# A two-layer graph attention kernel: the order of work inside a pipeline step is rewritten on three engines

## The chip, the cores and the metric

The kernel runs on one core of a Trainium2 chip. The metric is the device time of one execution in microseconds; the median of three runs of the kernel before is 667.15 us (666.98 to 670.65).

## The reference

```python
h = relu(layernorm(x))                                  # x: 6144 x 128
scores = where(adj > 0, h @ W0 @ input.T, -2**32 + 1)   # adj: 6144 x 6144 int32
x = x + softmax(scores / 0.07, axis=1) @ input
h = relu(layernorm(x)) ; z = h @ W1
e = leaky_relu(z @ a_src [:, None] + z @ a_dst [None, :], 0.2)
att = softmax(where(valid, e, -1e9), axis=1)            # valid: adj > 0 and sum(z) != 0
attention = where(att >= 1e-4, att, 0) * valid.sum(1)[:, None]
x = x + elu(z + attention @ z)
```

The adjacency has about two edges in a row, 151 MB of int32 in all, and is read once.

## The kernel before

The fast path works on 48 row tiles of 128 rows, in 12 blocks of B = 4 tiles. A tile's adjacency comes in three loads of 1 MB (SP, L705) into a ring of 5. ScalarE turns each into signs (`convert`, L848), TensorE folds them with powers of two into one bank of 128 x 512 numbers (`fold`, L1412), and VectorE takes the largest of each bank (`find`, L1004). From these the columns of a block's edges are decoded and listed, one-hot matrices between rows and edges are made (`make_R`, `make_RT`), the neighbours' rows of the input are gathered by GpSimd (`neighbours`, L797, 12 gathers a block), scored, softmaxed and summed (`attend`), normed, projected and stored as records in tables in HBM. After all blocks a second layer gathers records (L805, three thirds of a table, 48 gathers each) and computes layer two.

The pipeline is written by hand. There are 17 steps n. In step n a block of loads n is taken in, while block b1 = n-1 is decoded and gets its one-hots and its gathers, b2 = n-2 is scored and softmaxed, b3 = n-3 is attended, and b4 = n-4 is projected and recorded. Each engine runs its own list of these pieces, in the order in which the program calls them; `more(k)` puts k of a step's 12 loads (below called load 0 to load 11 of the step) between them: a `convert` each on ScalarE, a `fold` each on TensorE. A piece waits on semaphores, and everything behind it on its engine waits too. A later step's pieces never pass an earlier step's.

Pieces spoken of below: on VectorE `decode` (L1013 to L1025), `differences` (L1163, L1166), `list_columns` (L1031 to L1044, ends by releasing `deg_r`), `spread_lists` (L1050 to L1055), `shares` (L1172, L1174, makes RTp for `attend`), `ends_of_rows` (L1063 makes `below` for `make_R`), `columns_of_edges` (L1075 to L1086, gives GpSimd the indices, `idx_r`), `score` (L1115), `centre`, `normalise` (L1152 to L1157), `record`. On ScalarE `keep_R` (L877) and `keep_RT` (L886) copy the one-hots out of the banks, `exponent` (L897) stands between `centre` and `normalise`, `hidden_x` (L857) and `hidden` (L910) are four activations each. On TensorE `attend` (L1505, L1507), `make_R` (L1446), `edges_lists` (L1470, feeds `columns_of_edges`), `make_RT` (L1459), `spread` (L1424, feeds `score`), `edge_shares` (L1492).

GpSimd's list is: the 12 neighbour gathers of a block each step; from step 8 on also 12 record gathers from the first third, each four of them behind a count of folds of the next step; then, behind the gathers of block 10, 8 records, 12 records of the second third (these wait for the last fold of all), the 12 gathers of the last block 11, 28 and 4 more records, then a wait for the last table store, and 56 more records.

Of the kernel before, what the change touches and what calls it, by code (L numbers as in the profile page):

```python
# [415 lines left out]
def fast_path(nc, x, adj, inp, w0, w1, a, out, overflow):  # L416
# [50 lines left out]
    with ctx:  # L467
# [35 lines left out]
        exp_i = sb("exp_i", [P, B * NKEY], I32)  # L503
# [188 lines left out]
        with nc.Block() as block:  # L692
# [146 lines left out]
            def _(act):  # L839
# [79 lines left out]
                for n in range(NB + 5):  # L919
# [67 lines left out]
            def _(dve):  # L987
# [19 lines left out]
                def decode(b):  # L1007
# [10 lines left out]
                    for level in range(LEVELS):  # L1018

                        ts(exp_i[:, 0:w], code_f[:, 0:w].bitcast(I32), 23, None, ALU.logical_shift_right)  # L1020
                        link(ts(top_i[:, 0:w], code_f[:, 0:w].bitcast(I32), 0x7F800000, None, ALU.bitwise_and))
                        stt(cand[:, 0:size, level, :], exp_i[:, 0:w].rearrange("p (b e) -> p b e", b=size), float(FOLD),  # L1022
                            col_f[:, 0:w].rearrange("p (b e) -> p b e", b=size), ALU.mult, ALU.add)
# [202 lines left out]
                for n in range(NB + 5):  # L1226
# [6 lines left out]
                    if 0 <= b3 < NB:  # L1233
                        shares(b3)
                    if 0 <= b1 < NB:
                        list_columns(b1)
                    if 0 <= b4 < NB:
                        record(b4)
                    if 0 <= b1 < NB:
                        spread_lists(b1)  # L1240
                    if 0 <= b2 < NB:
                        split_g(b2)
                    if 0 <= b1 < NB:
                        ends_of_rows(b1)
                    if 0 <= b2 < NB:
                        score(b2)
                    if n < NB:
                        find(n, 0)
                    if 0 <= b2 < NB:
                        pieces_of_scores(b2)  # L1250
                    if n < NB:
                        find(n, 1)
                    if 0 <= b1 < NB:
                        columns_of_edges(b1)
                    if 0 <= b3 < NB:
                        add_attention(b3)
                    if 0 <= b2 < NB:
                        centre(b2)
                    if 0 <= b3 < NB:
                        norms(b3)  # L1260
                    if n < NB:
                        find(n, 2)
                    if 0 <= b2 < NB:
                        normalise(b2)
                    if n < NB:
                        find(n, 3)
                    if n == 0:
# [6 lines left out]
                    if 0 <= b2 < NB:  # L1274
                        rows_without_edges(b2)
                        differences(b2)
# [120 lines left out]
            def _(pe):  # L1397
# [18 lines left out]
                def spread(b, t):  # L1416
# [3 lines left out]
                    pe.wait_ge(RT_r, RPARTS[b + 1])  # L1420
# [7 lines left out]
                def first_edges(b):  # L1428
# [3 lines left out]
                    wait(pe, rec_r, b - 2)  # L1432
# [30 lines left out]
                def edges_lists(b):  # L1463

                    pe.wait_ge(R_r, RPARTS[b + 1])
                    pe.wait_ge(lists3_r, b + 1)
                    for t in range(SIZES[b]):
# [74 lines left out]
                for n in range(NB + 5):  # L1542
# [6 lines left out]

                    if 0 <= b3 < NB:  # L1550
# [4 lines left out]
                    if 0 <= b4 < NB:  # L1555
                        turn_hid(b4)
                    more(1)
                    if 0 <= b4 < NB:
                        project_hid(b4)
                    more(2)  # L1560
                    if 0 <= b3 < NB:
                        if b3 == 0:
                            pe.wait_ge(mean_kept, 1)
                        attend(b3)
                    if 0 <= b1 < NB:
                        first_edges(b1)
# [3 lines left out]
                    more(1)  # L1570
                    if 0 <= b2 < NB:
                        spread(b2, 1)
                        spread(b2, 2)
                        spread(b2, 3)
                    more(1)
# [91 lines left out]
```

## Time and profile before

| | |
|---|---|
| median of 3 runs | 667.15 us (666.98 to 670.65) |
| the profiled execution's own time | 668.12 us |
| its span | 666.6 us |
| granted TensorE clock, mean of the span | 0.806 |
| busy: PE / DVE / ACT / POOL | 60% / 74% / 61% / 43% |

The loads end at about 450 us, the first layer's last record is stored at about 545 us, and from 587 us on VectorE alone is nearly always busy with layer two. Times in the rows are counted from the start of the span.

### The profile page before, as it was taken

What the parts mean: (1) busy time and instruction counts of PE and PEld (TensorE: products, weight loads), DVE (VectorE), ACT (ScalarE), POOL (GpSimd) and SP (SyncE); (2) the same over time, 40 slices, a digit from 0 to 9 for tenths busy, and PEclk for the clock granted to TensorE, in tenths of its full rate; (3) what the DMA queues carried; (4) which work ended last, traced back from release to release, by engine and by line L of the source; (5) the groups of instructions that cost most, each with busy time, mean ns of one, the idle gap of its engine ahead of it and who ended that gap; (6) DMA issues with size and microseconds to landing.
All of it is one profiled execution on the core that took longest, in us unless ns stands there. A gap on an engine that the chain in (4) does not pass through costs nothing.

```text
span 666.6 us, 9873 instructions
## 1 busy us (share of the span) xinstructions
PE 399.5 (60%) x3043; PEld 274.6 (41%) x3043; DVE 490.8 (74%) x2173; ACT 407.2 (61%) x424; POOL 286.5 (43%) x329
## 2 busy tenths in 40 slices
PE   3146174757878787777868685765561621536654
PEld 1012032435554555444636363544450521536653
DVE  0006949798989898987989896979865513679994
ACT  6247579777898989979998988974220110022232
POOL 6000042240606060605147574747777777777000
PEclk9666587979797979988989998978875655657777
DMA  8999979999999999999999999961222232234222
GB/s 330 401 425 420 418 250 392 374 354 368 361 349 402 393 403 382 406 412 378 344 408 395 401 398 410 395 252 52 69 69 56 70 101 53 54 85 132 86 80 82
DMA packets 37479, 186.78 MB, mean 280 GB/s; under 512 B 7856, under 2 KB 8112, under 8 KB 18864
## 3 DMA queue, kind: packets, MB, share of 16 engines
q1 hardware_dynamic: 28208, 167.02, 64.0%
q0 software_dynamic: 9216, 19.11, 9.6%
q8 instruction: 25, 0.41, 0.2%
q14 instruction: 30, 0.25, 0.1%
HBM read 179.73 MB, written 6.37 MB: 279 GB/s over the span
## 4 chain that ended last, share of the span: by engine, by line
DVE 47%; PE 12%; POOL 12%; issue 11%; DMA 9%; ACT 8%; DVEq 0%; SPq 0%; POOLq 0%; ACTq 0%
DMA arena<-in_adj 8%; POOL arena L805 6%; PE K L1412 4%; ACT arena L848 4%; DVE keys L1004 3%; DVE G L1115 3%; ACT R_all L877 2%; DVE RTp L1174 2%; POOL X L797 2%; POOL arena L797 2%; DVE stats L1189 1%; DVE stats L1212 1%; DVE cand L1034 1%; DVE cand L1022 1%; POOL E L805 1%
## 5 line engine op out<-in xcount | busy, mean ns | idle before, releaser
L848 ACT ACTIVATE arena<-arena,half_c 128x2048 fp8e4<-128x2048 int32 x144 | 282.0, 1998 | 41.7 <-DMA arena<-in_adj 33.4
L797 POOL DMA_INDIRECT X<-in_L_gnn_input,idx_all x132 | 125.9, 953 | 279.9 <-DVE idx_near L1086 243.0
L1412 PE MATMUL K<-arena,bits 128*128 128x512 fp8e4 x576 | 167.1, 430 | 23.2 <-ACT arena L848 23.1
L805 POOL DMA_INDIRECT arena<-table,idx_near x96 | 92.8, 967 | 29.9 <-issue 29.0
L1412 PEld LDWEIGHTS K<-arena,bits 128*128 128x128 bf16 x576 | 59.5, 108 | 94.1 <-ACT arena L848 30.5
L1004 DVE MAX8 keys<-K 128x8 int32<-128x128 f32 x192 | 42.3, 281 | 56.9 <-PE K L1412 56.8
L805 POOL DMA_INDIRECT E<-table,idx_near x48 | 45.8, 955 | 15.4 <-issue 14.3
L1410 PE MATMUL K<-key_add,key_one 128*128 128x512 bf16 x48 | 20.8, 433 | 46.0 <-ACT arena L848 23.8
L1505 PE MATMUL W<-X,RTp 128*128 128x128 f32 x240 | 37.6, 298 | 4.6 <-DVE RTp L1174 4.3
L877 ACT CAST R_all<-G 128x512 fp8e4<-128x512 f32 x36 | 19.8, 587 | 30.6 <-PE G L1446 30.6
L1424 PE MATMUL G<-g,R_all 128*128 128x128 bf16 x324 | 26.1, 232 | 18.5 <-DVE g L1137 9.6
L1505 PEld LDWEIGHTS W<-X,RTp 128*128 128x128 f32 x240 | 33.8, 212 | 8.1 <-issue 7.8
L973 ACT ACTIVATE above<-above,zero_c 128x24 f32<-128x24 f32 x6 | 1.9, 314 | 52.8 <-DVE above L1342 52.8
L1424 PEld LDWEIGHTS G<-g,R_all 128*128 128x128 fp8e4 x324 | 21.4, 104 | 28.2 <-DVE g L1137 14.5
L1492 PE MATMUL SB<-mi,R_all 128*128 128x6 bf16 x144 | 5.7, 168 | 42.3 <-DVE mi L1157 42.2
L910 ACT ACTIVATE hid<-x_all,shift,rstd 128x128 f32<-128x128 f32 x48 | 19.8, 481 | 16.8 <-DVE shift L1224 16.7
L1115 DVE SCALAR_TENSOR_TENSOR G<-G,X 128x128 f32<-128x128 f32 x99 | 26.1, 323 | 3.1 <-PE G L1424 3.0
L1410 PEld LDWEIGHTS K<-key_add,key_one 128*128 128x128 bf16 x48 | 4.8, 99 | 54.5 <-issue 27.2
L1538 PE MATMUL W<-w_sb,hid_t 128*128 128x128 f32 x96 | 24.0, 342 | 3.7 <-ACT hid_t L917 3.7
L1492 PEld LDWEIGHTS SB<-mi,R_all 128*128 128x128 fp8e4 x144 | 4.6, 101 | 47.6 <-DVE mi L1157 47.6
L1075 DVE TENSOR_TENSOR ohs_all<-slot_of,SA 128x192 bf16<-128x192 bf16 x12 | 4.2, 354 | 24.4 <-PE SA L1470 24.4
L1174 DVE TENSOR_TENSOR RTp<-RT_all,SB 128x1536 f32<-128x1536 fp8e4 x12 | 21.0, 1753 | 0.4
(253 smaller groups left out, 975.9 us busy)
## 6 DMA issues: line engine op xcount, KB each, us to landing
arena<-in_adj SPq DMA_DIRECT2D x144, 1024.0 KB, 9.9
table<-hs SPq DMA_DIRECT2D x12, 262.0 KB, 8.8
hs<-table SPq DMA_DIRECT2D x12, 262.0 KB, 2.6
E<-in_L_gnn_input SPq DMA_DIRECT2D x1, 3072.0 KB, 25.8
out_x<-x_all SPq DMA_DIRECT2D x12, 256.0 KB, 2.0
x_all<-in_x SPq DMA_DIRECT2D x1, 2560.0 KB, 19.3
X<-in_L_gnn_input,idx_all POOLq DMA_INDIRECT x132, 5.4
arena<-table,idx_near POOLq DMA_INDIRECT x96, 2.5
```

The lines of the kernel that those rows point to most:

```text
L797: pool.indirect_dma_start(out=x_of(b)[:, e, :], out_offset=None, in_=inp, in_offset=bass.IndirectOffsetOnAxis(ap=idx_all[:, at:at + 1], ax ...
L805: pool.indirect_dma_start(out=E[g][:, t, :], out_offset=None, in_=tables[g], in_offset=bass.IndirectOffsetOnAxis(ap=idx_near[:, t, g:g + 1 ...
L848: nc.scalar.activation(sign[:, load % RING, :], ring[:, load % RING, :], ACT.Sign, bias=half_c[:], scale=1.0, saturate=False).then_inc(sig ...
L877: nc.scalar.copy(R_all[:, bass.ds(FROM[b] * G + i, width), :], one_hot_bank(i // 4)[:, 0:width * P].rearrange("p (e r) -> p e r", r=P), sa ...
L1004: last = nc.vector.max(keys[:, b % 2, u, q, :], K[tile % 2][:, q * w:(q + 1) * w])
L1115: last = stt(prod, prod, 1.0, x_of(b)[:, e, :], ALU.mult, ALU.mult, accum_out=s_e[:, b % 2, e:e + 1])
L1174: tt(RTp[:, 0:n_e], RT_all[:, edges(b), :], p_e[:, 0:n_e].unsqueeze(2).broadcast_to([P, n_e, P]), ALU.mult).then_inc(RTp_r, 1)
L1410: mm(bank_[:], key_one[:], key_add[:], start=True, stop=False)
L1412: last = mm(bank_[:], bits[:, third * TB + j, :], sign[:, load % RING, j * FOLD:(j + 1) * FOLD], start=False, stop=(third == G - 1 and j = ...
L1424: last = mm(spread_bank(t)[:, g * P:(g + 1) * P], R_all[:, (FROM[b] + t) * G + g, :], g3[:, c, t, :], start=(c == 0), stop=(c == PIECES - 1))
L1505: mm(att_of(b)[:, t * D:(t + 1) * D], RTp[:, e, :], x_of(b)[:, e, :], start=(g == 0), stop=False)
L1538: mm(W1[:, t * D:(t + 1) * D], hid_t[:, t, :], w_sb[:, 1, :], start=True, stop=True)
```

## The change

The pieces are the same, but each engine's list within a step is rewritten. VectorE makes the lists and one-hots of b1 first, and scores b2 near the end of the step; `differences` of a block moves from the end of one step to just behind the next `decode`. The removed `exp_i` operation was a shift; the multiply behind it now takes the unshifted exponent with a smaller constant. Four waits change with the order: `spread` waits for the RT of the block behind its own, `make_R` for the score of the step before, and `edges_lists` takes over `first_edges`' wait on `rec_r`.

```diff
@@ ScalarE
+                    more(1)
                     if 0 <= b3 < NB:
                         exponent(b3)
                     more(1)
                     if 0 <= b4 < NB:
-                        hidden(b4)
+                        keep_turned(b4)
+                    if 0 <= b2 < NB:
+                        keep_turned_x(b2)
                     more(2)
                     if 0 <= b3 < NB:
                         exponent_of_edges(b3)
                     if 0 <= b4 < NB:
-                        keep_turned(b4)
+                        keep_h(b4)
                     more(1)
-                    if 0 <= b1 < NB:
-                        hidden_x(b1)
-                    if 0 <= b4 < NB:
-                        keep_h(b4)
                     if 0 <= b2 < NB:
                         keep_high(b2)
-                    more(6)
+                    more(2)
                     if 0 <= b1 < NB:
                         keep_R(b1)
                     more(1)
                     if 0 <= b1 < NB:
                         keep_RT(b1)
-                        keep_turned_x(b1)
                     more(1)
+                    if 0 <= b1 < NB:
+                        hidden_x(b1)
+                    more(3)
+                    if 0 <= b3 < NB:
+                        hidden(b3)
@@ VectorE, decode
-                        ts(exp_i[:, 0:w], code_f[:, 0:w].bitcast(I32), 23, None, ALU.logical_shift_right)
                         link(ts(top_i[:, 0:w], code_f[:, 0:w].bitcast(I32), 0x7F800000, None, ALU.bitwise_and))
-                        stt(cand[:, 0:size, level, :], exp_i[:, 0:w].rearrange("p (b e) -> p b e", b=size), float(FOLD),
+                        stt(cand[:, 0:size, level, :], top_i[:, 0:w].rearrange("p (b e) -> p b e", b=size),
...
@@ VectorE, the list of a step (without its ifs)
-  decode(b1) shares(b3) list_columns(b1) record(b4) spread_lists(b1) split_g(b2) ends_of_rows(b1) score(b2)
-  find(n,0) pieces_of_scores(b2) find(n,1) columns_of_edges(b1) add_attention(b3) centre(b2) norms(b3)
-  find(n,2) normalise(b2) find(n,3) rows_without_edges(b2) differences(b2)
+  decode(b1) differences(b3) list_columns(b1) spread_lists(b1) shares(b3) ends_of_rows(b1) find(n,0)
+  record(b4) split_g(b2) add_attention(b3) columns_of_edges(b1) find(n,1) norms(b3) score(b2)
+  pieces_of_scores(b2) find(n,2) rows_without_edges(b2) centre(b2) find(n,3) normalise(b2)
@@ TensorE, waits
-                    pe.wait_ge(RT_r, RPARTS[b + 1])
+                    pe.wait_ge(RT_r, RPARTS[min(b + 2, NB)])
...
-                    wait(pe, spread_used, FROM[b])
+                    if b > 0:
+                        wait(pe, spread_used, FROM[b - 1])
@@ TensorE, the list of a step (without its ifs; 1, 2, 12 are more(...))
-  edge_shares(b3) 1 project_hx(b2) turn_hid(b4) 1 project_hid(b4) 2 attend(b3) first_edges(b1) 1 spread(b2,0)
-  1 spread(b2,1..3) 1 make_R(b1) turn_hx(b1) edges_lists(b1) rows(b2) make_RT(b1) 5
+  1 turn_hid(b4) edge_shares(b3) 1 project_hx(b2) project_hid(b4) 2 first_edges(b1) 1 attend(b3) 1 make_R(b1)
+  1 edges_lists(b1) make_RT(b1) 1 spread(b2,0..2) 2 spread(b2,3) 12 turn_hx(b1) rows(b2)
```

ScalarE, from the copy of g to the exponent, a step in the middle, before:

```order
L870 CAST g<-W 128x512
L848 ACTIVATE arena<-arena,half_c 128x2048 x6
L877 CAST R_all<-G 128x512 x3
L848 ACTIVATE arena<-arena,half_c 128x2048
L886 CAST RT_all<-G 128x512 x3
L864 COPY hx_t<-W 128x512
L848 ACTIVATE arena<-arena,half_c 128x2048
L897 ACTIVATE ex<-sc,zero_c 128x64
```

and now:

```order
L869 CAST g<-W 128x512
L847 ACTIVATE arena<-arena,half_c 128x2048 x2
L876 CAST R_all<-G 128x512 x3
L847 ACTIVATE arena<-arena,half_c 128x2048
L885 CAST RT_all<-G 128x512 x3
L847 ACTIVATE arena<-arena,half_c 128x2048
L856 ACTIVATE hx<-x_all,shift_x,rstd_x 128x128 x4
L847 ACTIVATE arena<-arena,half_c 128x2048 x3
L909 ACTIVATE hid<-x_all,shift,rstd 128x128 x4
L847 ACTIVATE arena<-arena,half_c 128x2048
L896 ACTIVATE ex<-sc,zero_c 128x64
```

The copy of R stood behind load 9 of the step and stands behind load 6; between it and the exponent there were two conversions and a copy, and there are six conversions and both groups of four activations.

TensorE at the same place, before:

```order
L1424 MATMUL G<-g,R_all 128x128 x9
L1410 MATMUL K<-key_add,key_one 128x512
L1412 MATMUL K<-arena,bits 128x512 x4
L1446 MATMUL G<-below,step_of 128x512 x3
L1515 MATMUL W<-ident,hx 128x128 x4
L1470 MATMUL SA<-lists,R_all 128x33 x12
```

and now, from the last piece of `attend`:

```order
L1507 MATMUL W<-mean_b,no_row 128x128
L1411 MATMUL K<-arena,bits 128x512 x4
L1445 MATMUL G<-below,step_of 128x512 x3
L1409 MATMUL K<-key_add,key_one 128x512
L1411 MATMUL K<-arena,bits 128x512 x4
L1470 MATMUL SA<-lists,R_all 128x33 x12
```

`make_R` stood behind the `spread` of the block in front, and stands behind its `attend` and one fold. GpSimd's and SP's lists are as they were.

## Rows read from the trace of the kernel before

**Rows 1.** Windows: us, then busy us of each engine, clock, DMA share, GB/s.

```profile
212.80:247.30 34.50, 26.51 (x208) 17.75 (x207) 31.09 (x151) 31.71 (x33) 11.47 (x13) 0.90 1.01 399
```

**Rows 2.** Timeline of VectorE: a later start of decode; columns: start us, us, what.

```profile
314.33 0.47 DVE L1013 CAST code_f<-keys 128x128 f32<-128x128 int32 x1
```

**Rows 3.** Timeline of VectorE in one step, 212.5 to 248 us.

```profile
214.43 0.73 DVE L1031 MAX8 lists<-cand 128x8 f32<-128x96 f32 x4
...
217.91 0.15 DVE L1095 COPY src_all<-SA 128x4 f32<-128x4 f32 x1
...
219.07 0.19 DVE L1050 TENSOR_SCALAR pen_all<-above 128x64 bf16<-128x64 f32 x1
...
220.00 0.69 DVE L1135 TENSOR_TENSOR g_r<-W,g 128x512 f32<-128x512 f32 x1
...
221.79 1.75 DVE L1063 TENSOR_TENSOR below<-iota_b,SA 128x1536 bf16<-128x1536 bf16 x1
...
231.22 0.35 DVE L1075 TENSOR_TENSOR ohs_all<-slot_of,SA 128x192 bf16<-128x192 bf16 x1 [1.47 <-PE SA L1470]
...
242.74 0.22 DVE L1163 TENSOR_REDUCE mie<-SB 128x24 f32<-128x72 f32 x1
...
243.22 0.47 DVE L1013 CAST code_f<-keys 128x128 f32<-128x128 int32 x1
...
244.05 0.23 DVE L1020 TENSOR_SCALAR exp_i<-code_f 128x128 int32<-128x128 int32 x1
244.19 0.22 DVE L1021 TENSOR_SCALAR top_i<-code_f 128x128 int32<-128x128 int32 x1
...
247.24 1.75 DVE L1174 TENSOR_TENSOR RTp<-RT_all,SB 128x1536 f32<-128x1536 fp8e4 x1
```

**Rows 4.** Timeline of ScalarE in the same step.

```profile
214.44 1.63 ACT L857 ACTIVATE hx<-x_all,shift_x,rstd_x 128x128 f32<-128x128 f32 x4
...
216.92 11.47 ACT L848 ACTIVATE arena<-arena,half_c 128x2048 fp8e4<-128x2048 int32 x6
229.00 1.65 ACT L877 CAST R_all<-G 128x512 fp8e4<-128x512 f32 x3 [0.62 <-PE G L1446]
...
236.68 0.35 ACT L897 ACTIVATE ex<-sc,zero_c 128x64 f32<-128x64 f32 x1 [0.18 <-DVE sc L1146]
```

**Rows 5.** Timeline of TensorE: attend of one block in mid stream, and after the loads.

```profile
216.79 0.83 PE L1505 MATMUL W<-X,RTp 128*128 128x128 f32 x6
...
464.39 1.62 PE L1505 MATMUL W<-X,RTp 128*128 128x128 f32 x6 [3.12 <-DVE RTp L1174]
...
470.12 0.17 PE L1435 MATMUL SA<-deg,tri_lt 128*128 128x12 bf16 x1
```

**Rows 6.** Timeline of ScalarE in step 1: the first long wait of the stream.

```profile
82.38 2.00 ACT L848 ACTIVATE arena<-arena,half_c 128x2048 fp8e4<-128x2048 int32 x1 [7.06 <-PE K L1412]
```

**Rows 7.** Timeline of ScalarE: loads 6 and 9 of the last block of loads.

```profile
432.15 2.00 ACT L848 ACTIVATE arena<-arena,half_c 128x2048 fp8e4<-128x2048 int32 x1 [0.78 <-DMA arena<-in_adj]
...
441.50 2.00 ACT L848 ACTIVATE arena<-arena,half_c 128x2048 fp8e4<-128x2048 int32 x1 [1.14 <-DMA arena<-in_adj]
```

**Rows 8.** Timeline of GpSimd: gathers of block 10, and the first record after the last store.

```profile
449.14 0.95 POOL L797 DMA_INDIRECT X<-in_L_gnn_input,idx_all  x1 [6.64 <-DVE idx_near L1086]
545.34 0.95 POOL L805 DMA_INDIRECT arena<-table,idx_near  x1 [0.89 <-DMA table<-hs]
```

**Rows 9.** Timeline of VectorE: score, normalise of the last block, and its layer two.

```profile
505.98 0.30 DVE L1115 SCALAR_TENSOR_TENSOR G<-G,arena 128x128 f32<-128x128 f32 x1 [7.90 <-DMA arena<-in_L_gnn_input,idx_all]
...
516.30 0.21 DVE L1152 TENSOR_REDUCE code_f<-ex 128x4 f32<-128x64 f32 x1
...
587.24 0.58 DVE L1297 TENSOR_TENSOR g<-ohs_all,arena 128x384 bf16<-128x384 bf16 x1 [9.41 <-DMA arena<-table,idx_near]
```

**Rows 10.** Windows: attend of the same step, and a later stretch; columns as in rows 1.

```profile
216.80:220.40 3.60, 3.60 (x35) 3.59 (x35) 3.26 (x20) 3.60 (x3) 0.00 (x0) 1.00 1.01 396
...
241.30:245.50 4.20, 4.20 (x26) 3.01 (x27) 3.94 (x21) 3.40 (x3) 3.23 (x4) 0.50 1.02 399
```

More of the change, by code:

```diff
@@ L1233, in _ @@
                     if 0 <= b3 < NB:
+                        differences(b3)
+                    if 0 <= b1 < NB:
+                        list_columns(b1)
+                        spread_lists(b1)
+                    if 0 <= b3 < NB:
                         shares(b3)
                     if 0 <= b1 < NB:
-                        list_columns(b1)
+                        ends_of_rows(b1)
+                    if n < NB:
+                        find(n, 0)
                     if 0 <= b4 < NB:
                         record(b4)
-                    if 0 <= b1 < NB:
-                        spread_lists(b1)
                     if 0 <= b2 < NB:
                         split_g(b2)
+                    if 0 <= b3 < NB:
+                        add_attention(b3)
                     if 0 <= b1 < NB:
-                        ends_of_rows(b1)
+                        columns_of_edges(b1)
+                    if n < NB:
+                        find(n, 1)
+                    if 0 <= b3 < NB:
+                        norms(b3)
                     if 0 <= b2 < NB:
                         score(b2)
-                    if n < NB:
-                        find(n, 0)
-                    if 0 <= b2 < NB:
                         pieces_of_scores(b2)
[L1251 to L1260, printed above, removed]
                     if n < NB:
@@ L1263, in _ @@
                     if 0 <= b2 < NB:
-                        normalise(b2)
+                        rows_without_edges(b2)
+                        centre(b2)
                     if n < NB:
                         find(n, 3)
+                    if 0 <= b2 < NB:
+                        normalise(b2)
                     if n == 0:
@@ L1431, in first_edges @@
                     wait(pe, lists_kept, b)
-                    wait(pe, rec_r, b - 2)
                     n_e = SIZES[b] * G
@@ L1466, in edges_lists @@
                     pe.wait_ge(lists3_r, b + 1)
+                    wait(pe, rec_r, b - 2)
                     for t in range(SIZES[b]):
@@ L1548, in more @@
                             fold(n, c)
+                    more(1)
+                    if 0 <= b4 < NB:
+                        turn_hid(b4)
                     if 0 <= b3 < NB:
@@ L1564, in _ @@
                         attend(b3)
+                    more(1)
                     if 0 <= b1 < NB:
-                        first_edges(b1)
+                        make_R(b1)
+                    more(1)
+                    if 0 <= b1 < NB:
+                        edges_lists(b1)
+                        make_RT(b1)
                     more(1)
@@ L1569, in _ @@
                         spread(b2, 0)
-                    more(1)
-                    if 0 <= b2 < NB:
                         spread(b2, 1)
                         spread(b2, 2)
+                        more(2)
                         spread(b2, 3)
-                    more(1)
+                    more(12)
                     if 0 <= b1 < NB:
-                        make_R(b1)
                         turn_hx(b1)
-                        edges_lists(b1)
                     if 0 <= b2 < NB:
                         rows(b2)
-                    if 0 <= b1 < NB:
-                        make_RT(b1)
-                    more(5)
                     if n == 0:
```

12 lines of the change are left out of this document (4 added, 8 removed).

## The prediction

> **What bounds the kernel now.** I read the windows by step first, then the timelines of one step, then the chain of waits at the end. A step in mid stream lasts 34.5 us [rows 1]: from a `decode` at 243.22 [rows 3] the one two steps on stands at 314.33 [rows 2], 71.1 us = 2 x 34.5 and one hiccup of 2.1. Within it no engine is idle for long: ScalarE is busy for 31.7 us, VectorE for 31.1 and idle for only 1.47, the transfers' share is 1.01 [rows 1, 3]. In the last steps of the stream the loads bind: ScalarE waits for each of them, and loads 6 and 9 of the last block arrive at 432.15 and 441.50, 3.12 us each [rows 7].
>
> Behind the stream the chain belongs to GpSimd. It waits 6.64 us for the indices of block 10, starts its gathers at 449.14, and from there to 545.34 issues 76 gathers (12 + 8 + 12 + 12 + 28 + 4) with 0.89 of waiting at the end: (545.34 - 0.89 - 449.14) / 76 = 1.254 us each [rows 8]. The last 56 records follow, and layer two waits for those until 587.24 [rows 9]; behind that VectorE alone runs to the end. So the end moves with GpSimd, and GpSimd moves with the indices of block 10. The table's last store is only 0.89 behind it: the second chain is nearly as long.
>
> **The change, part by part.** Take T for the start of `decode`.
>
> *The shift removed.* The shift at 244.05 delays the next operation by 0.14 us [rows 3]; three levels give 0.4 us a step on VectorE. Worth nothing where another engine ends the step.
>
> *The middle of the stream.* VectorE to RTp: `decode` and the first multiply of `shares` 247.24 - 243.22 = 4.0, less 0.4; `differences` 243.22 - 242.74 = 0.5; `list_columns` 217.91 - 214.43 = 3.5; `spread_lists` 220.00 - 219.07 = 0.9; RTp itself 1.75 [rows 3]. RTp is there at T + 10.3, `below` at T + 12.0. But `make_R` now stands on TensorE behind `attend` (3.6 us, [rows 5, 10]) and a fold (0.9, by a load's four matmuls, an estimate from the 0.83 of six in rows 5): the first R is there at about T + 15.2, with 0.4 for its matmul. From there ScalarE has, up to the exponent: two groups of one-hot copies (2 x 1.6), six conversions at 11.47 / 6 = 1.91, two groups of four activations (2 x 1.6) [rows 4]: 17.7 us, T + 32.9. The exponent 0.35 and `normalise` 1.4 (an estimate: six chained operations of about 0.2 each, as the small ones of rows 3 are) end the step at T + 34.6. All seven pieces are links of one loop over three engines, and `normalise` is followed by the next `decode`. VectorE's own work would end at 34.5 - 1.5 - 0.4 = 32.6, so it now waits two us before `normalise`. **The step stays 34.6**, and the shift and the 1.47 us won on VectorE are lost there. Its bounds: 32.6 if the loop does not close, 36.7 below. ScalarE's conversions come out more evenly (never more than three in a row, six before), so the hiccup of 2.1 should go.
>
> *The start.* In step 1 ScalarE waits 7.06 us before load 9 [rows 6], for TensorE, which waits for `list_columns`. Now ScalarE stands before `keep_R` there, after load 6: two more conversions (3.8 us) and one group of activations (1.6) come behind the wait instead of before it, less the 3 us that VectorE waited later anyway. I take +2 for it (between 0 and 5.4), and +1 for the next two steps together. With the hiccup gone, the stream enters its last, transfer-bound steps 1 us later than now.
>
> *The last block of loads.* The bytes are the same, so the last load arrives as now, at 441.50 + 2 x 3.12 = 447.7. But the indices of block 10 hang on R, and R on the copy behind load 6 instead of load 9: 432.15 + 2.0 to convert, 1.65 to copy, about 1.6 for a fold and the lists, 2.4 for `columns_of_edges`: 439.8, where now it is 449.14 - 0.3. With the 1 us of the start **the gathers of block 10 begin at about 440.5, 8.6 us earlier**. They end at 440.5 + 15.0 = 455.5; the records behind them wait for the last fold, at 447.7 + 1 + 2 + 1 = 451.7, and that is past. Hence GpSimd's row of 76 gathers ends at 440.5 + 95.3 = 535.8.
>
> *The last store.* The gathers of block 11 end 8.6 us earlier, so its score may start at 497.4 instead of 505.98 [rows 9]. In the new order the attention and the norms of block 10 come before this score and not behind it. By the working of the step above VectorE is there near 500.5: the last fold 451.7 and 4 for the rest of the step, 31 for a step without loads, 14 for the part of the next before the score. From the score to `normalise` it was 10.3 us [rows 9]; without those two pieces (4.4, an estimate from four and fourteen of the operations of rows 3) it is about 7 (the exponent is then waited for). So the store, 39.4 us behind the score now [rows 8, 9], is 36 behind it: 536.5, beside 535.8. That keeps the 0.9 us of waiting about as it is. Both chains agree: layer two begins 8.6 to 9 us earlier.
>
> *GpSimd's and SP's queues* have no piece moved. Records of block b4 are stored behind a step's loads as before. `record` itself comes 5 us later in a step, and nothing waits for it there but `edges_lists`, later still. The relaxed wait of `make_R` is worth nothing here: the score that it named is long past in the old place. `spread`'s longer wait costs nothing while `keep_RT` (T + 20.2) is before `score` (T + 23).
>
> **Sum**, against the profiled execution's 668.1: -8.6 for the indices, -0.4 for what is left of the wait for the store: 659.1. The median of the runs stands 1.0 below the profiled execution: **658**.
>
> **The rivals.**
>
> 1. *The loop does not close.* If the first R comes earlier than I count (`attend` partly hidden, conversions ahead), the six steps of the middle fall toward VectorE's 32.6 or what the transfers allow; the share of 1.01 [rows 1] speaks against much. At 33.5 a step: 6 x 1.1 = 6.6 more, 651.5, since the part that the transfers bind then begins that much earlier.
>
> 2. *Slower: `attend` runs at half clock in its new place.* It now follows a wait of TensorE for RTp (from about T + 9 to T + 10.3), and everything that ends the step hangs on it. At the full clock (1.00, 2.4 GHz) its 3.6 us stand in [rows 5, 10]; behind a wait of 3.12 us it took 470.12 - 464.39 = 5.7 at the lower clock, as [rows 5] show, and a stretch at 0.50 (1.2 GHz) is found within a step too [rows 10]. Then the loop is 34.6 + 2.1 = 36.7, six steps give back 12.6, and the time is 670.6. It decides from 1.4 us a step on (8.6 / 6), that is from a step of 36.0; beyond 2.6 us a step, with the other matmuls of the loop slow too, it is 1% slower. The waits that I count in the new order are shorter (the longest 2.5 us, before a fold), so it is the less likely. The Trainium skill (TensorE: Matmul & The Clock Gate, section "HAM oscillation — how this bites in real kernels") says that waits between groups of matmuls put the array back to half its clock; by that rule a loop with TensorE's waits in it would be the 36.7 case. The low stretch of rows 10 agrees with it for a long wait.
>
> 3. *The second chain is longer than counted*: the last store is late by more than GpSimd's row, because block 10 is finished before block 11 is scored. Each us above 536.5 is a us of the gain; at 5 us, 663. The whole gain is lost only at 545, an order behind which I find nothing.
>
> 4. *The change doesn't do what it says*: indices of block 10 held by something else than load 6 (a GpSimd record group behind a fold, say). Then the gain is the half of it or none: 663 to 667.
>
> **Chances and range.** The forecast 0.5, its own range 654 to 663; rival 1 0.17, around 651; rival 2 0.15, around 671; rivals 3 and 4 together 0.18, 661 to 667. A measurement of this kernel can tell about 1% from no change, so faster means under 660.5 and slower over 673.8. Faster: 0.4 of the forecast's 0.5, 0.17 and a little of rivals 3 and 4: 0.6. Slower: half of rival 2 and the unforeseen: 0.1. The range leaves a tenth on either side: 646 to 670.
>
> **What would show it.** In the profile after: `decode` to `decode` of 34 to 35 us in the middle, VectorE idle about 2 us before `normalise` for the exponent, and ScalarE idle 2 to 3 before the copy of R. The first gather of block 10 at 439 to 442. The 76 gathers in one row without a gap. The loads' last arrival within 2 us of now. The first layer's last store within 2 us of the end of GpSimd's row. I am wrong if the step is not 34.6, or if GpSimd waits between block 10's gathers and the last store, or if layer two takes another time than the 79 us from 587.24 to the end.

## The result, and the profile after: slower by 3%

| | before | after |
|---|---|---|
| median | 667.39 us (4 runs, 666.98 to 670.65) | 689.09 us (4 runs, 687.80 to 690.57) |
| ratio | | 1.031, 95% interval 1.029 to 1.034 |
| the profiled execution, its span | 668.1, 666.6 us | 687.8, 686.2 us |
| `decode` of block 3 begins | 174.25 us | 184.45 us |
| `decode` of block 11 begins | 458.51 us | 485.15 us |
| layer two's last records are there | 587.24 us [rows 9] | 607.24 us |

The forecast was 658 and its range ended at 670. The table splits the loss: 184.45 - 174.25 = 10.2 us come in the first steps, (485.15 - 184.45) - (458.51 - 174.25) = 16.4 in the eight steps after them, and 26.6 - 20.0 = 6.6 are won back behind them. Of the eight, the first six hold the whole 16.7 (225.56 us against 208.90); in the last two the loads bound the kernel before, and both kernels take 75 us. So the six steps that the forecast counted were the right number, and the length of one was not.

The eight steps. This is VectorE's timeline after, two starts of `decode` a step apart (start, duration, what):

```profile
222.06 0.23 DVE L1015 CAST code_f<-keys 128x128 f32<-128x128 int32 x1
...
259.65 0.23 DVE L1015 CAST code_f<-keys 128x128 f32<-128x128 int32 x1
```

A step lasts 37.6 us (37.5 to 37.7 in all eight, also where the loads bound before), where [rows 1] had 34.5. The windows of that step, columns as in [rows 1], in five pieces and as a sum:

```profile
222.20:232.20 10.00, 7.14 (x54) 4.33 (x54) 9.41 (x45) 10.00 (x11) 0.00 (x0) 0.99 1.00 404
232.20:237.40 5.20, 5.17 (x33) 5.19 (x34) 4.96 (x17) 1.72 (x1) 0.00 (x0) 0.69 1.01 400
237.40:246.70 9.30, 7.51 (x72) 4.24 (x70) 7.17 (x37) 8.03 (x11) 2.28 (x3) 1.00 0.75 286
246.70:251.30 4.60, 1.74 (x5) 0.72 (x6) 2.28 (x19) 4.60 (x5) 3.39 (x4) 0.76 0.99 330
251.30:259.80 8.50, 5.70 (x49) 3.62 (x48) 6.77 (x35) 7.13 (x8) 5.67 (x6) 0.93 1.01 401
sum 37.60, PE 27.26 PEld 18.11 DVE 30.59 ACT 31.48 POOL 11.35; mean PE 5.45 PEld 3.62 DVE 6.12 ACT 6.30 POOL 2.27
```

Every engine did the work it did before, and each has 6 us or more of idle time: nothing is full, so the step is a loop of waits. The second and the fourth piece are well below the full clock, 0.69 and 0.76 (and the start of the fifth, 0.93 in its mean). TensorE's timeline shows what ran there (in brackets the idle time before, and what ended it):

```profile
229.71 1.04 PE L1411 MATMUL K<-arena,bits 128*128 128x512 fp8e4 x4
232.23 1.62 PE L1505 MATMUL W<-X,RTp 128*128 128x128 f32 x6 [1.48 <-issue]
233.64 0.64 PE L1507 MATMUL W<-mean_b,no_row 128*128 128x128 f32 x2
234.07 1.48 PE L1505 MATMUL W<-X,RTp 128*128 128x128 f32 x6
...
235.60 0.83 PE L1505 MATMUL W<-X,RTp 128*128 128x128 f32 x6
236.27 0.39 PE L1507 MATMUL W<-mean_b,no_row 128*128 128x128 f32 x2
...
237.39 1.03 PE L1411 MATMUL K<-arena,bits 128*128 128x512 fp8e4 x4
238.25 0.59 PE L1445 MATMUL G<-below,step_of 128*128 128x512 bf16 x2
...
245.73 1.04 PE L1411 MATMUL K<-arena,bits 128*128 128x512 fp8e4 x4
249.62 1.91 PE L1411 MATMUL K<-arena,bits 128*128 128x512 fp8e4 x4 [2.86 <-ACT arena L847]
251.33 1.16 PE L1423 MATMUL G<-g,R_all 128*128 128x128 bf16 x9
```

Half of `attend` runs at 1.2 GHz: six matmuls take 1.62 and 1.48 us, then 0.83 at 2.4 GHz. From 232.23 to the fold at 237.39 that is 5.16 us, where the prediction had 3.6. The fold of load 9 takes 1.91 instead of 1.04, `spread(b2, 3)` behind it 1.16 instead of the 0.66 that one run below shows. ScalarE's timeline, and VectorE's near the end of the step:

```profile
238.67 1.65 ACT L876 CAST R_all<-G 128x512 fp8e4<-128x512 f32 x3 [4.75 <-PE G L1445]
...
247.11 5.77 ACT L847 ACTIVATE arena<-arena,half_c 128x2048 fp8e4<-128x2048 int32 x3
252.79 1.64 ACT L909 ACTIVATE hid<-x_all,shift,rstd 128x128 f32<-128x128 f32 x4
254.32 1.99 ACT L847 ACTIVATE arena<-arena,half_c 128x2048 fp8e4<-128x2048 int32 x1
257.68 0.35 ACT L896 ACTIVATE ex<-sc,zero_c 128x64 f32<-128x64 f32 x1 [1.37 <-DVE sc L1147]
```

```profile
252.53 0.30 DVE L1116 SCALAR_TENSOR_TENSOR G<-G,X 128x128 f32<-128x128 f32 x1 [3.56 <-PE G L1423]
...
257.42 0.22 DVE L1147 TENSOR_TENSOR sc<-sc,mi 128x64 f32<-128x64 f32 x1
257.57 0.88 DVE L1006 MAX8 keys<-K 128x8 int32<-128x128 f32 x4
258.37 0.20 DVE L1153 TENSOR_REDUCE code_f<-ex 128x4 f32<-128x64 f32 x1
```

Read backwards: `normalise` (258.37) needs the exponent, and the exponent not for ScalarE's own work, as predicted, but 1.37 us for `centre`. That hangs on the last tile of `score`, which stood 3.56 us for `spread(b2, 3)`, which stands on TensorE behind the fold of load 9, which waits for the conversion that begins at 247.11. VectorE was forecast to stand about 2 us before `normalise`; it stands before `score` instead. This chain is in every step, as the group of the score's line on the page shows (busy, mean ns of one, and idle before): 37.6 us for `spread` in all.

```profile
L1116 DVE SCALAR_TENSOR_TENSOR G<-G,X 128x128 f32<-128x128 f32 x99 | 25.8, 324 | 37.7 <-PE G L1423 37.6
```

The start: ScalarE in step 1, and in step 3, against [rows 6]:

```profile
84.23 1.81 ACT L876 CAST R_all<-G 128x512 fp8e4<-128x512 f32 x3 [13.38 <-PE G L1445]
```

```profile
150.51 0.30 ACT L901 ACTIVATE x_e<-d_e,zero_c 128x12 f32<-128x12 f32 x1 [6.14 <-DVE d_e L1167]
...
163.46 1.65 ACT L876 CAST R_all<-G 128x512 fp8e4<-128x512 f32 x3 [6.49 <-PE G L1445]
```

13.4 us with seven loads converted, where ScalarE stood 7.06 before the tenth load and 1.00 behind it. By step the start is 3.1 us longer in step 1 (34.48 against 31.39), 2.9 in step 2 and 4.1 in step 3 (`decode` to `decode`). In step 3 two waits of 6 us each; the transfers' share is 0.74 there (0.93 before).

The tail: GpSimd and layer two, against [rows 8] and [rows 9]:

```profile
469.27 0.95 POOL L796 DMA_INDIRECT X<-in_L_gnn_input,idx_all  x1 [0.42 <-DVE idx_near L1087]
...
565.56 0.95 POOL L804 DMA_INDIRECT arena<-table,idx_near  x1 [0.32 <-issue]
```

```profile
607.24 0.56 DVE L1296 TENSOR_TENSOR g<-ohs_all,arena 128x384 bf16<-128x384 bf16 x1 [8.76 <-DMA arena<-table,idx_near]
```

The gathers of block 10 begin with 0.42 of waiting instead of 6.64. Their indices come 468.69 - 447.56 = 21.1 us after the block's `decode`, 448.57 - 421.20 = 27.4 before. GpSimd has no wait for the last store now, but from the first gather to the 77th it is 96.3 us as before (96.2): the 0.89 won nothing. Layer two begins 20.0 us later, as the gathers (20.1).

### The profile page after: what moved, and what is told of

It is laid out like the page before. It is cut to its first block, busy times and chain, and to the rows that moved or that the text cites. A ratio compares the mean times of both kernels' runs of the same rounds, so it can differ in the third digit from the quotient of the medians.

```text
span 686.2 us, 9803 instructions
## 1 busy us (share of the span) xinstructions
PE 405.3 (59%) x3011; PEld 278.7 (41%) x3043; DVE 485.6 (71%) x2137; ACT 403.9 (59%) x424; POOL 286.0 (42%) x329
## 4 chain that ended last, share of the span: by engine, by line
DVE 25%; ACT 18%; issue 18%; PE 16%; POOL 15%; DMA 7%; another core or an unknown queue 1%; SPq 0%; ACTq 0%; DVEq 0%
ACT arena L847 12%; POOL arena L804 10%; DMA arena<-in_adj 7%; PE K L1411 7%; PE W L1505 5%; DVE keys L1006 2%; ACT hx L856 2%; POOL E L804 2%; POOL arena L796 2%; POOL X L796 2%; ACT R_all L876 2%; PE W L1507 1%; DVE G L1116 1%; ACT RT_all L885 1%; PE G L1423 1%
## 5 line engine op out<-in xcount | busy, mean ns | idle before, releaser
L1411 PE MATMUL K<-arena,bits 128*128 128x512 fp8e4 x576 | 169.6, 427 | 63.7 <-ACT arena L847 59.2
L1411 PEld LDWEIGHTS K<-arena,bits 128*128 128x128 bf16 x576 | 57.0, 108 | 93.7 <-ACT arena L847 37.6
L804 POOL DMA_INDIRECT E<-table,idx_near x48 | 46.7, 974 | 36.7 <-PE K L1411 24.5
L1505 PE MATMUL W<-X,RTp 128*128 128x128 f32 x240 | 48.2, 357 | 15.9 <-issue 15.0
L1116 DVE SCALAR_TENSOR_TENSOR G<-G,X 128x128 f32<-128x128 f32 x99 | 25.8, 324 | 37.7 <-PE G L1423 37.6
L1505 PEld LDWEIGHTS W<-X,RTp 128*128 128x128 f32 x240 | 43.6, 267 | 20.6 <-issue 20.6
L1423 PEld LDWEIGHTS G<-g,R_all 128*128 128x128 fp8e4 x324 | 23.9, 113 | 17.5 <-issue 17.2
L1538 PE MATMUL W<-w_sb,hid_t 128*128 128x128 f32 x96 | 25.6, 361 | 0.7 <-ACT hid_t L916 0.7
L1433 PE MATMUL SA<-deg,tri_lt 128*128 128x12 bf16 x12 | 2.2, 185 | 37.7 <-DVE deg L1045 37.7
L1409 PE MATMUL K<-key_add,key_one 128*128 128x512 bf16 x18 | 7.4, 413 | 24.7 <-ACT arena L847 24.4
L1064 DVE TENSOR_TENSOR below<-iota_b,SA 128x1536 bf16<-128x1536 bf16 x12 | 21.0, 1748 | 0.1
L1458 PE MATMUL G<-step_of,below 128*128 128x128 bf16 x144 | 12.0, 219 | 14.0 <-ACT RT_all L885 14.0
```

The costliest lines, as they stand in the source:

```text
L804: pool.indirect_dma_start(out=E[g][:, t, :], out_offset=None, in_=tables[g], in_offset=bass.IndirectOffsetOnAxis(ap=idx_near[:, t, g:g + 1 ...
L1064: tt(below[:, 0:n_e], iota_b[:].unsqueeze(1).broadcast_to([P, n_e, P]), SA[:, BG:BG + n_e].unsqueeze(2).broadcast_to([P, n_e, P]), ALU.is_ ...
L1116: last = stt(prod, prod, 1.0, x_of(b)[:, e, :], ALU.mult, ALU.mult, accum_out=s_e[:, b % 2, e:e + 1])
L1411: last = mm(bank_[:], bits[:, third * TB + j, :], sign[:, load % RING, j * FOLD:(j + 1) * FOLD], start=False, stop=(third == G - 1 and j = ...
L1423: last = mm(spread_bank(t)[:, g * P:(g + 1) * P], R_all[:, (FROM[b] + t) * G + g, :], g3[:, c, t, :], start=(c == 0), stop=(c == PIECES - 1))
L1505: mm(att_of(b)[:, t * D:(t + 1) * D], RTp[:, e, :], x_of(b)[:, e, :], start=(g == 0), stop=False)
```

## The experiments

The theory after the first look (A): the loop of 37.6 closes over two stretches of TensorE at 1.2 GHz and over the chain load 9, fold, `spread(b2, 3)`, score, which the prediction had left out. The rivals: only one of the two counts; the order alone is at fault and the clock is a by-product; or the loss is of the start.

**e1: the shift alone**, in the order of before.

```diff
- ts(exp_i[:, 0:w], code_f[:, 0:w].bitcast(I32), 23, None, ALU.logical_shift_right)
- stt(cand[...], exp_i[...], float(FOLD), col_f[...], ALU.mult, ALU.add)
+ stt(cand[...], top_i[...], float(FOLD) / (1 << 23), col_f[...], ALU.mult, ALU.add)
```

> The kernel before with only the shift removed (the exponents not shifted out), all orders as before. VectorE has 0.4 us less a step. Theory A (the shift's removal is harmless, it's the order that costs): 660 to 667.5 us, a step of 34.1 to 34.5 between decodes, because VectorE nearly fills the step before. Theory B (the new constant or the longer chain costs): slower than 668.

Measured: 665.52 us, ratio 0.995 (0.993 to 0.997). Its shortest steps are 34.07, 0.4 under those of before: in the old order the shift is worth its 0.4 us, as it would if VectorE's work is in the loop there. It is not what made the kernel slower.

**e2: the fourth spread ahead of the fold of load 9**, everything else as in the change.

```diff
                         spread(b2, 2)
-                        more(2)
+                        more(1)
                         spread(b2, 3)
```

> The changed kernel with one TensorE edit: the spread of a block's last tile stands before the fold of load 9 instead of behind it. Theory 'load 9': in the changed kernel the score of the last tile waits 3.56 us for this spread, that for the fold, and the fold for ScalarE's conversion of load 9, and this chain ends the step. Then the wait before the score's last tile goes, the conversions on ScalarE end the step, and the step falls from 37.57 to about 35.9: 674 us (670 to 678). Rival 'attend alone': the step is set only by attend and ScalarE's work behind the copies of R, and nothing is won: 688 to 690, step 37.5.

Measured: 667.71 us, ratio 0.999 (0.997 to 1.000): 21 us less than the change by moving nine matmuls ahead of one fold, and below the expected 670 to 678. TensorE, as above:

```profile
260.09 0.91 PE L1505 MATMUL W<-X,RTp 128*128 128x128 f32 x6 [1.45 <-issue]
...
263.74 1.03 PE L1411 MATMUL K<-arena,bits 128*128 128x512 fp8e4 x4
...
273.98 0.66 PE L1423 MATMUL G<-g,R_all 128*128 128x128 bf16 x9 [0.86 <-DVE G L1116]
```

The step is 34.56, the 34.6 of the prediction. The second chain is out of the loop, and more than expected happened: `attend` takes 263.74 - 260.09 = 3.65 us at a granted clock of 1.00, behind a wait as long as that of the change (1.45 here, 1.48 there). The total doesn't tell order from clock, but two of its steps, shown below, do.

**e3, e4, e7: fillers.** The order of the change, but TensorE does matmuls of 200 columns, whose result nobody reads, in its waits of steps 3 to 11: ahead of `attend` (e3, 22 in all), ahead of both (e4, 22 and 24), ahead of the fold of load 9 alone (e7, 24). In e3 and e4 a wait on `h_kept` ahead of the first fillers is added too.

```diff
+                    wait(pe, h_kept, b3)
+                    warm(W1, 8)        # e3, e4
                     if 0 <= b1 < NB:
                         first_edges(b1)
                     more(1)
+                    warm(W1, 14)       # e3, e4
                     if 0 <= b3 < NB:
...
                     if third == 0:
                         wait(pe, keys_used, tile - 1)
+                        if c == 9:
+                            warm(K[tile % 2], 24)   # e4, e7
```

> The changed kernel with short matmuls of 200 columns into the bank of attend, whose result nobody reads, 8 before first_edges and 14 before attend, in steps 3 to 11: TensorE has no idle time before attend. Theory 'clock': attend takes 5.16 us in the changed kernel because the granted clock falls to half in it (0.69 in its stretch); with the filling it takes 3.6, R comes 1.5 earlier, and the step falls by 1.5 from 37.57 to 36.0: 675 us (672 to 679). Rival: attend is slow for another reason (its operands, the bank, the DMA traffic): attend stays at 5.2 and the step at 37.5 or longer: 688 to 693.

> As the run with the filling before attend, and 24 more such matmuls into the bank of the fold of load 9, before that fold waits for its load, in steps 3 to 11. Theory 'clock': both slow stretches go (attend 3.6, fold and spread 1.4 instead of 3.3), and the step is the 34.6 of the prediction's sum, 34.4 to 35: about 662 us (658 to 667). Rival 'order': the chains cost their length at any clock, the step stays above 36: 675 or more.

> The changed kernel with 24 filler products of 200 columns into the key bank ahead of the fold of load 9 in steps 3 to 11, and none ahead of attend. Theory A (the loop of 37.6 us closes over the conversion of load 9, its fold, spread(b2, 3), and the score's last tile, and the half clock there is only part of it; attend stays at a granted clock near 0.7 and 5.2 us): the fold takes 1.0 and spread 0.7 us, the exponent comes 1.4 us earlier in its step, the step is 36.1 us and the total about 675 us, ratio 1.010. Theory B (one stretch at half clock brings the other: a shorter step keeps TensorE busier and attend is at full clock too): step 34.7, total 668 to 671 us, ratio 1.000 to 1.005. Theory C (nothing in the loop is at the clock): 689 us, ratio 1.031.

| | ratio (interval) | step in mid stream |
|---|---|---|
| e3 | 1.003 (1.001 to 1.005), 670.68 us | 34.8 to 36.1 |
| e4 | 1.003 (1.001 to 1.005), 670.01 us | 34.7 to 35.0, the last 36.0 |
| e7 | 1.007 (1.004 to 1.010), 672.15 us | five of 34.7 to 34.9, three of 36.4 to 36.6 |

Nothing is moved in these kernels and work is only added, and 17 to 19 us go: the clock is a cause, and no by-product. e3 came out below its range (672 to 679). e4's step is right, but its total is 8 us over the 662 expected. Its start is only 2.2 us earlier than that of the change (`decode` of block 3 at 182.23), and 2.6 us lie outside the profiled span (669.7 against a span of 665.5, 4.2 apart, where the change has 1.6); why they do isn't shown. In e7, Theory B of its expectation fits in five steps of eight, and the total is just above its range. The windows of such a step, in the same pieces as those of the change:

```profile
218.40:228.50 10.10, 7.20 (x54) 4.43 (x55) 9.52 (x45) 10.10 (x11) 0.07 (x1) 1.00 1.02 410
228.50:232.20 3.70, 3.64 (x32) 3.67 (x33) 3.53 (x15) 1.68 (x1) 0.00 (x0) 1.00 1.02 418
232.20:241.40 9.20, 7.41 (x72) 4.34 (x71) 8.45 (x39) 7.91 (x11) 2.16 (x3) 1.00 1.00 401
241.40:245.90 4.50, 3.81 (x39) 3.01 (x39) 2.53 (x20) 4.50 (x5) 3.50 (x4) 1.00 0.98 292
245.90:253.10 7.20, 4.46 (x33) 2.42 (x33) 6.72 (x33) 7.19 (x8) 5.46 (x6) 1.00 0.95 376
```

The two pieces that shrink are the second (5.2 to 3.7, `attend`) and the last (8.5 to 7.2, behind the fold of load 9): 2.8 of the 2.9 us. `attend` has no filler before it here; it waits 1.56 us and still has the clock at 1.00.

The clock also changes from step to step within one kernel, with nothing else in the program changed. In e2 the step that begins at 284.31 has a slow `attend`, and the next has not; TensorE, and the windows of the two steps:

```profile
294.64 1.23 PE L1505 MATMUL W<-X,RTp 128*128 128x128 f32 x6 [1.44 <-issue]
...
296.09 1.49 PE L1505 MATMUL W<-X,RTp 128*128 128x128 f32 x6
...
299.92 1.03 PE L1411 MATMUL K<-arena,bits 128*128 128x512 fp8e4 x4
```

```profile
284.31:320.50 36.19, 28.19 (x207) 17.68 (x206) 30.81 (x148) 31.37 (x33) 11.40 (x13) 0.91 0.98 383
320.50:355.06 34.56, 25.12 (x208) 15.79 (x206) 30.75 (x148) 31.36 (x33) 11.40 (x13) 1.00 1.00 394
```

`attend` takes 299.92 - 294.64 = 5.28 us there, and the step is 1.6 longer. The step of e2 from 389.78 (36.43) and the three long ones of e7 have a slow `attend` too (the last of the three is a load-bound step, 36.0 in e4 as well). In e3 it is never slow (0.91 for the first six matmuls in all eight steps), and the steps go with the second place: 36.1 in the four where the fold of load 9 takes 1.91 (one of the four is load-bound), 34.8 where fold and spread take 1.02 and 0.67, and 35.2 to 35.6 in the other three, where the fold takes 1.02 to 1.25 and the spread 1.1 to 1.2. In e4 the clock is 1.00 in all eight steps.

**e5, e8, e9: the start.** All three are e2 with one thing more. e5 and e9: ScalarE converts ten loads ahead of `keep_R` in step 1, instead of seven; in e5 TensorE also folds six instead of four ahead of `first_edges`. e8: `differences(0)` at the end of step 2, where it was before.

```diff
-                    more(2)
+                    more(5 if n == 1 else 2)    # ScalarE, ahead of keep_R: e5, e9
...
-                    more(2)
+                    more(4 if n == 1 else 2)    # TensorE, ahead of first_edges: e5
```

```diff
-                    if 0 <= b3 < NB:
+                    if 0 < b3 < NB:             # e8
                         differences(b3)
...
+                    if b2 == 0:
+                        differences(b2)
                     link.step()
```

> The changed kernel with spread(b2, 3) ahead of the fold of load 9 (as e2_spread_before_fold9, which stood at 0.9989 of the kernel before), and in step 1 alone ScalarE converts ten loads ahead of keep_R instead of seven, as the kernel before did, with TensorE folding six instead of four ahead of first_edges. Theory A (the start term: in step 1 ScalarE stood 13.38 us behind keep_R with seven loads converted, where the kernel before stood 7.06 and had ten): the second block's lists begin about 3 us earlier, near 104 us instead of 107, and all behind moves with it: about 664.5 us, ratio 0.994. Theory B (the lateness at the start is of the steps 2 and 3, whose steps grew 37.1 and 36.5, or the transfers catch up behind it): the total stays at 667 to 668, ratio 0.998 to 1.000. The locked step in the middle stays 34.6 by both.

> The changed kernel with spread(b2, 3) ahead of the fold of load 9 (0.9989 of the kernel before), and differences(0) at the end of step 2 where the kernel before has it, instead of in step 3; all other steps as in the change. Theory A (a part of the start term: in step 3 ScalarE stood 6.17 us behind the first block's differences with four loads converted, and the transfers with it, share 0.75): that wait goes or falls under 3 us, step 3 falls from 36.5 to 34.6 us or less and the total by 2 to 3 us, to about 665, ratio 0.995. Theory B (ScalarE then waits as much longer for keep_R, 6.86 us there now, whose chain runs over the one-hots alone): step 3 stays at 36 to 37 us and the total at 667 to 668, ratio 0.998 to 1.000.

> The changed kernel with spread(b2, 3) ahead of the fold of load 9, and in step 1 ScalarE converts ten loads ahead of keep_R instead of seven; TensorE's order is the change's (in e5_start_fix it folded six ahead of first_edges, and the indices of block 0 came 4.2 us later, at 92.6 instead of 88.4). Theory A (the lateness of step 1 is ScalarE's wait of 13.4 us with seven loads converted): keep_R stays near 84 to 86 us, decode of the second block comes at 103 to 105 us instead of 107, and the total is 2 to 3 us less, about 665, ratio 0.995. Theory B (the five places of the ring are full at seven to nine loads until TensorE folds more, so ScalarE waits for TensorE in place of keep_R): decode of the second block stays at 106 to 108, the total at 667 to 668.

| | ratio (interval) | `decode` of block 1 | of block 3 |
|---|---|---|---|
| e2 | 0.999 (0.997 to 1.000) | 107.05 | 180.62 |
| e5 | 0.996 (0.995 to 0.998), 666.19 us | 106.39 | 181.13 |
| e8 | 0.998 (0.995 to 1.000), 667.14 us | 107.87 | 182.27 |
| e9 | 0.990 (0.987 to 0.993), 661.14 us | 101.24 | 176.35 |

e5 showed nothing of what was asked, because the added folds made a new wait (its expectation had 664.5 or 667 to 668, and it lies between them); on TensorE:

```profile
83.94 0.61 PE L1409 MATMUL K<-key_add,key_one 128*128 128x512 bf16 x1 [3.32 <-DVE keys L1006]
84.34 3.62 PE L1411 MATMUL K<-arena,bits 128*128 128x512 fp8e4 x8
87.75 0.72 PE L1445 MATMUL G<-below,step_of 128*128 128x512 bf16 x2
```

The seventh fold needs a bank that VectorE has not read yet, and `make_R` stands behind it: 87.75 instead of the 83.50 of e9. Without those folds, ScalarE in e9 stands 6.74 us instead of 13.4:

```profile
82.27 2.00 ACT L847 ACTIVATE arena<-arena,half_c 128x2048 fp8e4<-128x2048 int32 x1 [6.74 <-PE K L1411]
84.18 1.63 ACT L876 CAST R_all<-G 128x512 fp8e4<-128x512 f32 x3
```

`keep_R` is hardly later (84.18, and 83.89 in e2), three loads more are converted, and step 1 is 6 us shorter (28.0 against e2's 34.0); all behind it follows. I had expected 2 to 3. e8 took half of its wait away (2.72 us left of 6.17), but `keep_R` then waited 10.83 instead of 6.86, and step 3 stayed at 36.6: Theory B.

**e6: the new order only at the end**, from step 11 on (with the spread of e2), the old order without the shift up to step 10. At the change-over `differences(8)` and `keep_turned_x(9)` have been done by the old order and are left out, and `hidden(7)` is added.

```diff
+                    if n < 11:
+                        ...                      # the pieces in the order of before
+                    else:
+                        ...                      # the pieces in the order of the change
```

> Shift left out; steps 0 to 10 in the order of the kernel before, steps 11 and on in the order of the change with spread(b2, 3) ahead of the fold of load 9. Theory A (the tail term of the prediction: the new order gives the indices of block 10 about 6 us earlier in its step, and the gathers, layer two and the end follow them): the indices of block 10 at about 437 us against 443.4 in e1_shift_alone, and the total about 659.5 us, ratio 0.986 (0.983 to 0.989). Theory B (the end is set by another chain, the records of the last block, or the step of the change-over itself costs what the indices gain): the indices come earlier, the total stays at 664 to 667, ratio 0.993 to 0.997.

Measured: 659.93 us, ratio 0.987 (0.984 to 0.989), as Theory A has it. But in its profile the indices of block 10 stand at 441.89, hardly ahead of the 442.85 of e1 (they had been expected at 437), and the two kernels had run on different chips. So three kernels ran once more, side by side:

> The same kernel as e1_shift_alone, beside e11 on one chip, since the two were measured on different ones. It is the base for the tail term: ratio 0.995 to the kernel before by both theories, about 665 us.

> The same kernel as e6_late_switch. Theory A (the tail term is real: within its step the indices of block 10 come 5.4 us earlier than in e1, T + 21.7 against T + 27.2, and the end follows): 4 to 7 us below e10, ratio 0.985 to 0.989. Theory B (the profiled executions, 662.3 and 660.9, told the truth, and most of the difference of the medians is between chips): 0 to 2 us below e10, ratio 0.992 to 0.995.

> The same kernel as e9_step1_conversions, on the same chip as e10 and e11. If its 0.9901 stands it is 3 us below e10 and 1 to 2 us above e11; if its step 1 of 28.0 us was one lucky execution, the decode of the second block comes at 104 to 107 us again and the total is that of e2, 0.999.

| | ratio (interval) | `decode` of block 10 | its indices |
|---|---|---|---|
| e10 (as e1) | 0.992 (0.989 to 0.995), 663.08 us | 415.34 | 441.96 |
| e11 (as e6) | 0.986 (0.983 to 0.989), 660.66 us | 420.12 | 441.29 |
| e12 (as e9) | 0.989 (0.986 to 0.992), 661.74 us | 420.83 | 441.65 |

GpSimd at the first gather of block 10, in e10 and in e11:

```profile
442.53 0.94 POOL L797 DMA_INDIRECT X<-in_L_gnn_input,idx_all  x1 [6.87 <-DVE idx_near L1085]
```

```profile
441.86 0.94 POOL L796 DMA_INDIRECT X<-in_L_gnn_input,idx_all  x1 [0.43 <-DVE idx_near L1116]
```

Within the step the new order is 26.6 - 21.2 = 5.4 us earlier, yet only 0.7 us earlier from the start of the span: the step begins 4.8 us later in these executions. In e11 GpSimd then waits 1.40 us for the last table store (0.86 in e10), and layer two begins at 580.05 in both. The medians differ by 2.4 us and their intervals just overlap, which is between the two theories (4 to 7, and 0 to 2). e9's start held (`decode` of block 1 at 101.12).

## Why the prediction was wrong, point by point

**The step that failed is "the step stays 34.6".** It measured 37.6. Two errors of about 1.4 us each are in it, and the last 0.2 come from the exponent to the next `decode` (259.65 - 257.68 = 1.97 us, 1.75 forecast).

- *`attend` 3.6 us.* Measured 5.16, granted clock 0.69. RTp was ready at T + 10.06 (10.3 forecast), but the copy of R began at 238.67 - 222.06 = T + 16.6 instead of T + 15.2. This is rival 2's mechanism in its place: priced at 2.1 us it would have given 36.7 and 670.6. I had argued it away by the length of the waits. Measured, the lower clock cost 1.5 us here and not 2.1.
- *One chain to the exponent.* The prediction followed only ScalarE's work behind the copy. The other way into the exponent, from the conversion of load 9 over fold, spread and score, stands nowhere in it. Since the copy came 1.4 late, so did that conversion, and with 0.9 for the fold and 0.5 for the spread at half clock this chain came out 1.37 us behind the other, which is the exponent's wait. At the full clock the two would have tied, by the same numbers (an estimate). It is a chain that the new order made: in the old one the last three spreads stand ahead of the fold of load 6.

That the two are tied together is what e2 and e7 show: either the order or 24 fillers, at the second place alone, gives 34.6 to 34.9 and brings `attend` back to 1.00 in most steps (five of the first seven in e2, five of eight in e7), where the change has it slow in every one. With only the first place filled (e3) the steps lie between 34.8 and 36.1, as the second place is at the lower clock or not. So the chance of 0.15 for rival 2 was too low, and its size of 2.1 us a step too small for the whole loop (3.0 measured, from 34.6 to 37.6): the prediction itself named other slow matmuls of the loop as the way past 1%, and that is what came. The Trainium skill (TensorE: Matmul & The Clock Gate, section "HAM oscillation — how this bites in real kernels") was weighed in the prediction and set aside; its rule pointed the right way for the change, though the page's own case has longer waits than these. The measurements are not one-sided: with a wait of 1.5 us ahead of it, `attend` was at 0.69 in the change, at 1.00 in most steps of e2 and e7 and slow in the others. What decides is not settled by these runs.

**The term of the start** was mis-sized: +3 forecast, +10.2 measured. Step 1 alone was near (+2 forecast, +3.1 measured); steps 2 and 3 together were not (+1 forecast, +6.9 measured). By the runs, 4.3 us of the 10.2 come from ScalarE's standing behind `keep_R` with seven loads instead of ten (e2 against e9: 180.62 to 176.35, and 107.05 to 101.24 at block 1; the ratios moved by 0.9%, 6 us). The prediction counted what came behind the wait (5.4) and took 3 back for a later wait of VectorE. 3.8 more go with the place of the fourth spread (184.45 to 180.62, the change against e2). The 2.1 us left between e9 and the kernel before are a sum: step 1 is 3.4 us shorter in e9 (27.98 against 31.39), step 2 is 1.8 longer, and step 3 is 3.5 longer (37.12 against 33.67). Of step 3, e8 shows only that its two waits trade against each other; its cause stays open.

**The hiccup** went as forecast: the eight steps are within 0.2 us of each other. But that is luck: it was to go because the conversions come more evenly, and in e2 and e7, with the same spread of conversions, single steps are 36.2 to 36.6 again. Those are the steps whose `attend` is at the lower clock, which in the change is every step, and e4 at 1.00 has none ahead of its last step. Whether the clock made the 2.1 us of the kernel before too isn't shown (`attend` takes 0.91 and 0.83 there).

**The tail** was right as a mechanism and too large. In its step the indices come 6.3 us earlier (21.1 against 27.4), GpSimd's 6.64 of waiting is 0.42, and the profile gave back 6.6 behind the stream. But the forecast 440.5 for the first gather was not reached by any kernel (441.86 was the earliest on record here), and e10, in the old order without the shift, stood at 442.53, 6.6 us earlier than the kernel before (449.14): of the 8.6 us, most were to be had without the new order, and the same-chip comparison leaves it 2.4, not well resolved. Rivals 3 and 4 did not show in the change: no wait for the last store, and layer two keeps its distance. Rival 3's second chain is near, though: in e11 it holds GpSimd for 1.40 us, and its profiled execution gains nothing on e10's.

**The shift** at nothing was right for the new order by its argument (VectorE stands idle there: 3.56 us before the end of `score`), and e1 shows that it is worth 0.4 us a step in the old. It was not undone within the change itself.

With both repairs (e9, e12) the new order stands at 661.1 and 661.7, 3 us over the forecast's 658: that is what the order can do mostly at the full clock and without the second chain. That it comes so near is in part luck, since the start and the tail were both sized wrong. The lowest medians are those of e6 and e11, ratio 0.987 and 0.986 to the kernel before, but their intervals overlap those of e9 and e12, and on the same chip e11 and e12 are 1.1 us apart.

## What to carry to other kernels

Where a step is closed by a loop over several engines, list every way into its last operation, not only the one that the new order was made for, and price each matmul of the loop at half the clock wherever a wait stands ahead of it; if the forecast then changes sign, the order isn't safe. A piece that a loop needs should not stand on an in-order engine behind work that comes later (a fold whose load is converted late), and in the first steps of a pipeline an early wait costs the loads that were queued behind it.

## What the runs showed of the hardware

- The granted clock can close a loop on itself. A step of 37.6 us had two stretches at 0.69 and 0.76, and it repeated within 0.2 us for eight steps; with 24 more matmuls in one of its waits (2.2 us of TensorE, e7), five of the eight steps went to 1.00 and 34.7 to 34.9 us. More work made those 2.9 us shorter.
- A wait of equal length had different effects: 1.48 us ahead of `attend` with 1.62 us for six matmuls in the change, 1.45 us with 0.91 and then 0.83 in e2, and in another step of e2 1.44 us with 1.23 and then 1.49.
- What a slow stretch costs where it comes alone: 1.6 us a step for `attend` (e2, 36.19 against 34.56), 1.2 for the fold of load 9 and the spread (e3, 36.05 against 34.83).
